# One wait for gather and scatter together in the expert loop of a routed layer

## The reference

```python
E, K, CAP = 64, 8, 128               # experts, experts per token, slots per expert
topk_idx, topk_w = _route(x, gate_weight, e_bias)
# the tokens are sorted by expert; pos is a token's place in its expert's queue
xe = zeros((E, CAP, H)).at[sorted_e, pos].set(tok_sorted, mode='drop')
h  = silu(einsum('ech,efh->ecf', xe, w1)) * einsum('ech,efh->ecf', xe, w3)
ye = einsum('ecf,ehf->ech', h, w2)
vals = where(pos < CAP, ye[sorted_e, pos], 0.0)
out = segment_sum(vals * flat_w, flat_t, num_segments=T)      # add back to the tokens
shared = (silu(x @ shared_gate.T) * (x @ shared_up.T)) @ shared_down.T
return out + shared
```

## Time and profile before

| | |
|---|---|
| median of 3 executions | 5789.74 us |
| the profiled execution itself | 5806.9 us |
| its span, first to last instruction | 5805.1 us |
| first to last Pool instruction start in `small_experts` | 1174.10 to 1447.29 us |
| Pool instructions there | 64 gathers, 64 scatters, 128 pauses |

### The profile page before, as it was taken

The page is one execution under the profiler, slowest core; times in us unless marked ns, Lnnn a source line. Parts: engine busy times, 40 slices in busy tenths (PEclk is TensorE's granted clock), DMA queues, the critical chain, the costliest instruction groups (busy, mean ns, idle before and its releaser), DMA issues. The chain is left out here.

```text
span 5805.1 us, 287455 instructions
## 1 busy us (share of the span) xinstructions
PE 4256.0 (73%) x120752; PEld 3384.4 (58%) x120752; DVE 3164.7 (55%) x11531; ACT 1915.3 (33%) x5257; POOL 2416.9 (42%) x4365
## 2 busy tenths in 40 slices
PE   6989966054799887734898999204886998858987
PEld 5877743032566676612677886102554887757866
DVE  3545569232344577779454555533332656775556
ACT  3544421011344333323454452001222553325632
POOL 3434410476333466600333441066885445653310
PEclk9989977555899756656899998557997998988989
DMA  3000000433100111100000001112332000000001
GB/s 80 4 7 18 18 20 25 88 63 56 31 0 0 23 27 27 26 8 0 2 0 8 19 19 31 35 49 65 72 78 55 0 1 19 18 10 2 0 1 29
DMA packets 375650, 149.79 MB, mean 26 GB/s; under 512 B 218848, under 2 KB 365280, under 8 KB 375040
## 3 DMA queue, kind: packets, MB, share of 16 engines
q1 hardware_dynamic: 334416, 104.91, 7.5%
q0 software_dynamic: 40960, 40.93, 4.3%
HBM read 101.34 MB, written 43.87 MB: 25 GB/s over the span
## 5 line engine op out<-in xcount | busy, mean ns | idle before, releaser
L850 DVE TENSOR_REDUCE rowmax<-ps 128x16 f32<-128x1024 f32 x512 | 627.2, 1225 | 797.8 <-PE ps L536 797.8
L554 PE MATMUL ps<-qT,kblock 32*64 32x64 f32 x36864 | 987.4, 237 | 26.4 <-issue 20.2
L418 POOL TENSOR_TENSOR vareps<-meanvar,eps 128x1 f32<-128x1 f32 x576 | 110.3, 191 | 1818.8 <-DVE negmean L829 1818.8
L554 PEld LDWEIGHTS ps<-qT,kblock 32*64 32x64 f32 x36864 | 818.8, 141 | 75.3 <-issue 27.3
L536 PE MATMUL ps<-kblock,qT 32*64 32x128 f32 x16384 | 829.5, 305 | 9.7 <-issue 9.0
L578 PE MATMUL ps<-v,probT 64*64 64x64 f32 x36864 | 801.5, 235 | 10.2 <-ACT probT L754 3.5
L578 PEld LDWEIGHTS ps<-v,probT 64*64 64x64 f32 x36864 | 718.2, 148 | 110.9 <-issue 107.0
L754 ACT ACTIVATE probT<-ps 128x1024 f32<-128x1024 f32 x512 | 524.5, 1024 | 738.3 <-PE ps L565 738.0
L455 POOL TENSOR_TENSOR kblock<-kT,key_scale 128x512 f32<-128x512 f32 x576 | 601.5, 1044 | 85.1 <-ACT kT L734 56.8
L536 PEld LDWEIGHTS ps<-kblock,qT 32*64 32x64 f32 x16384 | 501.4, 143 | 148.3 <-issue 120.1
L637 PE MATMUL ps<-consts,xn 128*128 128x128 f32 x576 | 193.4, 336 | 366.7 <-ACT xn L739 156.8
(11 more groups left out here) (311 smaller groups left out, 9406.1 us busy)
## 6 DMA issues: line engine op xcount, KB each, us to landing
ctxT<-in_ctxT SPq DMA_DIRECT2D x256, 64.0 KB, 1.8
held<-in_g_w SPq DMA_DIRECT2D x16, 836.0 KB
ctxT<-in_ctxT SPq DMA_DIRECT2D x256, 32.0 KB, 1.8
table<-prob SPq DMA_DIRECT2D x32, 256.0 KB, 2.3
x_dram<-x_res SPq DMA_DIRECT2D x16, 512.0 KB, 6.3
x_res<-x_dram SPq DMA_DIRECT2D x16, 512.0 KB, 7.2
x_res<-in_x SPq DMA_DIRECT2D x8, 512.0 KB, 7.1
x_res<-in_e_w SPq DMA_DIRECT2D x64, 64.0 KB
```

The lines of the kernel that those rows point to most:

```text
L554: mm = nc.tensor.matmul(out, k.kblock[rows, buf, h, S * b:S * b + S], k.qT[rows, buf, S * b:S * b + S], start=not softmax or (first and h ...
L850: nc.vector.tensor_reduce(spread, heads, AX.X, ALU.max).then_inc(k.max_raw, 1)
```

## The change

In the Pool stream of `small_experts` the waits of the scatter move to the front of the step, ahead of the waits of the gather. One pause per step (`pause_gather`) follows all of them, then the gather, then the scatter. The pause of the scatter (`pause_add`) is gone. The single pause stands outside the condition for the gather, so it also runs in steps 64 to 67, which have a scatter alone. There are 68 pauses in place of 128. The waits' values are the same.

```diff
             def step(it, u, ends):
                 par = u % 2
+                if active(it, 4, ends):
+                    t, b = it - 4, par
+                    pool.wait_ge(k.e_scaled, t + 1)
+                    if positive(16 * t):
+                        pool.wait_ge(k.e_added, 16 * t)
                 if active(it, 0, ends):
-
                     pool.wait_ge(k.e_index, it + 1)
                     if positive(it - 3):
                         pool.wait_ge(k.e_xT_psum, it - 3)
                         pool.wait_ge(k.e_col, it - 3)
-                    pool_pause(k, pool, k.pause_gather, 5, it)
+                pool_pause(k, pool, k.pause_gather, 5, it)
+                if active(it, 0, ends):
                     nc.gpsimd.indirect_dma_start(
                         out=xe[:, u, :], out_offset=None, in_=r.table,
                         in_offset=bass.IndirectOffsetOnAxis(ap=k.e_gidx[:, u, 0:1], axis=0),
                         bounds_check=T + P - 1, oob_is_err=True).then_inc(k.e_x_ready[u], 16)
                 if active(it, 4, ends):
-                    t, b = it - 4, par
-
-                    pool.wait_ge(k.e_scaled, t + 1)
-                    if positive(16 * t):
-                        pool.wait_ge(k.e_added, 16 * t)
-                    pool_pause(k, pool, k.pause_add, 6, t)
                     nc.gpsimd.indirect_dma_start(
                         out=k.x_dram, out_offset=bass.IndirectOffsetOnAxis(ap=k.e_sidx[:, b, 0:1], axis=0),
                         in_=ys[:, b, :], in_offset=None, bounds_check=T + P - 1, oob_is_err=True,
```

## The result

The changed kernel takes 5875.99 us (median of 4 runs, 5874.1 to 5887.55) against 5789.56 us before (median of 4). The ratio is 1.0158, 95% interval 1.0142 to 1.0174: 86 us slower by the medians, where 5880.3 us and 91 us were forecast, inside the range of 5861 to 5897.

What follows compares the result with a forecast made beforehand. The expert loop was taken as bound by Pool's pause, scatter and landing, 4.17 us per step. Terms 1.34 + 0.20 - 0.03 = 1.51 us, times 60, add 90.6 to 5789.7: 5880.3 us, range 5861 to 5897.

Steps and rivals of the forecast that it cites:

- The missing pause: Scatter's own pause on Pool, 60 fewer in the expert loop; it stood inside the landing time, so gain 0.
- The gather in the ring: Gather on Pool now delays the scatter behind it by 1.34 us per step, bounds 1.31 and 1.40.
- the ring: Pool's repeating chain in the expert loop: pause, scatter, its landing, next pause; 4.17 us per step before the change.
- The waits behind the landing: Long satisfied waits now between the scatter's landing and Pool's pause cost 0.2 us per step, bounds 0 and 0.3.
- The landing, -0.03: Scatter's start to landing, 3.43 us, shortens by 0.03 us as its packets part from the weight load's; bounds -0.08 and 0.
- Nothing behind becomes late: The later gather makes no TensorE or VectorE work late, its expert's scatter being due four steps later; cost 0.
- a landing over 3.6 us: Sign in the changed profile: this long from scatter to Pool's pause would speak for data queueing behind the gather.
- few us: Sign: the prediction is wrong if another stage's length changes by more than this.
- the one with data queued behind the gather: Scatter's data wait behind the gather's in one software queue; landing up to 0.6 us later, 5916 us; 8 in 100.
- The rival by which the two would be generated side by side: On Pool, a scatter directly behind a gather starts at once, costing nothing; 5785 to 5790 us; 4 in 100.
- The rival by which the network has to finish in the step of its gather: The later gather becomes the expert loop's bound, some 10 us a step, 6140 us; 2 in 100.

## Why the prediction was right

Point by point, with the mean sizes measured:

1. *The missing pause, 0*: right. With the scatter ahead of the gather, the landing wait last and still one pause less, the ratio is 0.9992, interval to 1.0001. The median gap from the pause to the first DMA is 0.74 us as before.
2. *The gather in the ring, +1.34*: 1.39 us in the changed kernel (1.38 in the median). The row with a scatter behind a gather, which the trace of before lacked, came out at the upper end of the bounds (1.31 to 1.40). The 1.34 held for the very first pair (1179.73 to 1181.07 us); from then on the gather itself takes 1.07 us and not 1.03, as it did behind a scatter before, and that is 0.04 us of the difference. One late step of 1.86 us adds 0.01. Taking the gather out of the ring (scatter first) gave 1.35 us back.
3. *The waits behind the landing, +0.20*: right. The table gives it by the two landings: Pool's pause was 0.05 us ahead of VectorE and is now 0.17 us behind, 0.22 us. Turning the waits round gave 0.20 us back in the changed kernel (5.72 to 5.525) and 0.21 us with the scatter first (4.37 to 4.16).
4. *The landing, -0.03*: the landing at VectorE went from 3.45 to 3.42. The parting that I gave as the reason can be seen in one period. In 40 slices of 0.1 us from 1410 us (scatter at 1409.31) the packets of the gather and of the weight load end at 1411.0, and the scatter's stand alone from 1411.4 to 1412.1; before, scatter and weight load made one stretch of 1.4 us. That the parting is what shortened the landing is not shown: the size is small, and the landing at VectorE is 3.43 to 3.49 us in the other kernels with the gather in front, on other chips.
5. *Nothing behind becomes late*: right. Scatters are paced by the landing in the steady part (56 of Pool's pauses released by it). TensorE now waits for the gathers, 59 times and 143.2 us in all between 1184 and 1530 us, but off the ring. In one period (pause at 1303.86 us) it took the gather up 2.80 us after its start and was through with L2017 5.56 us behind the pause; 2.81 and 5.57 were forecast.

The row of point 4, busy tenths of the DMA engines in the changed kernel from 1410 us:

```profile
DMA  4875212421000069799950000000000000000000
```

The sizes add up: 1.39 + 0.22 - 0.03 - 0.04 = 1.54 us, the rise of the mean period, where 1.51 was forecast. The -0.04 is the two late steps of the profile before, for which the prediction had no term. The loop grew by 91.2 us, forecast 90.6. That it came within 1 us is partly luck: terms 2 and 3 were 0.05 and 0.02 us too small, and the late steps took more than half of it away. The sum was made on the loop; the whole came out 4 us lower than forecast by the medians, within the spread of the changed kernel's runs.

Two signs in the prediction were badly set. It wrote 3.4 us from scatter to pause and 1.8 us of idle, and called a landing over 3.6 us a sign of the queue, though its own terms 3 and 4 make 3.43 + 0.20 - 0.03 = 3.60 us. Measured are 3.59 us and 2.00 us; only the row of VectorE, at 3.42 us, tells the landing from the waits behind it. And the rest of the program changed by 24 us between the two profiles, more than the "few us" that should have spoken against it; in the part with most of it TensorE's granted clock differs too (0.79 and 0.80), so this sign could not tell the change from the clock.

Of the rivals, the one with data queued behind the gather fails by the narrow gather and by the landing, which is 3.40 us at Pool's pause both before the change and with a gather directly in front of the scatter (landing wait last). With two gathers in front at most some 0.08 us of it could be there. With two gathers in the landing time VectorE sees the landing 3.61 us after the scatter's start, 0.16 us later than before; why is open, and Pool sets the pace there.

The rival by which the two would be generated side by side fails by 1.39 us from gather to scatter, and by 1.38 and 1.32 us between the three DMAs of the kernel with two gathers. The Trainium skill ("DMA: Bandwidth & Descriptors", section "Anatomy of one DMA — SWDGE (gpsimd) path") calls descriptor generation "small, variable" and puts the dispatch at about 50 ns. Here it is not small: a gather occupies Pool for 1.07 us and a scatter for 1.59 us.

The rival by which the network has to finish in the step of its gather fails by the period of 5.72 us, where it put some 10.

## What to carry to other kernels

When a chain of dependent DMAs sets the pace, look for what stands between the landing of one and the issue of the next: each indirect DMA put there cost its whole generation on every turn here, and the same DMA issued just behind, in the landing time, cost nothing until Pool was full. Put the wait that ends last at the end of the list, since satisfied waits behind it cost 0.2 us here. Merging two waits holds back the work that needed only the earlier one. Here that was harmless as long as this work was issued second (ratio 0.9992), because its result is only needed steps later; issued first, it also held up the other.

## What was not expected of the hardware

- The gap of 0.74 us between a pause and the indirect DMA after it is 0.36 us when Pool was busy all the while. The 0.38 us, which I take for work of the sequencer, are paid behind a pause that had to wait, also with that wait as the last one ahead of the pause (0.74 us). An idle figure such as 0.34 us before the pause therefore understates the slack, which was 0.76 us.
- A gather of 128 rows takes 1.38 us of Pool's time to the next scatter with 768 bytes a row and with 512 bytes a row alike.
